# Two expert layers in a two-layer transformer: gates broadcast through DRAM instead of spread by matmuls

## The reference

```
x = x + attention0(layernorm(x))     # 16 heads of 8, rotary
x = x + moe0(layernorm(x))           # one shared and 7 routed experts, top 2, width 352
x = x + attention1(layernorm(x))
x = x + layer1_ffn(layernorm(x))     # relative attention, then 32 experts, top 4, width 128
```

```
# moe0, w[..., e] the normalised softmax gate (1 for the shared expert)
out = out + w[..., e:e+1] * einsum(silu(h @ g.T) * (h @ u.T), d)
# the second expert layer
h   = relu(einsum('bsd,edh->bseh', x2, keys))
out = einsum('bseh,ehd,bse->bsd', h, values, gate)
```

## Time and profile before

| what | us |
|---|---|
| median of 3 runs | 2346.78 (2344.66 to 2352.80) |
| profiled execution | 2339.8 |
| its span, first to last instruction | 2338.0 |
| `experts0`, first key matmul to accumulator copy | 473.4 to 691.7 |
| `experts1`, first spread matmul to accumulator copy | 2116.3 to 2329.3 |
| PE, DVE, ACT, POOL busy | 2140.5, 1581.1, 1303.8, 655.6 |

### The profile page before, as it was taken

How to read it: one execution, slowest core, us unless ns; L and a number is a source line. 1 busy time by engine, 2 the same in 40 slices (tenths; PEclk the granted TensorE clock), 3 DMA queues, 4 the chain that set the end, 5 groups by cost and what they waited for, 6 DMA issues and landing times.

```text
span 2338.0 us, 45544 instructions
## 1 busy us (share of the span) xinstructions
PE 2140.5 (92%) x14816; PEld 1312.2 (56%) x14816; DVE 1581.1 (68%) x2143; ACT 1303.8 (56%) x2269; POOL 655.6 (28%) x596
## 2 busy tenths in 40 slices
PE   4799999599984999999599999999999999959998
PEld 2344444367762344444277777777776777746765
DVE  4899997555545999996665666666666566666665
ACT  1588888155541688888244444444444444425675
POOL 1000000267761000000222222232322222226886
PEclk8799999599996899999699999999999999969999
DMA  7344442200005344442500100000000010100000
GB/s 235 112 117 118 106 121 70 60 30 19 10 0 156 100 111 122 107 117 73 168 13 24 33 26 24 24 24 24 24 24 24 25 34 24 35 28 19 20 20 27
DMA packets 85495, 142.87 MB, mean 61 GB/s; under 512 B 17152, under 2 KB 54016, under 8 KB 85120
## 3 DMA queue, kind: packets, MB, share of 16 engines
q1 hardware_dynamic: 85440, 142.19, 22.5%
HBM read 107.91 MB, written 36.04 MB: 62 GB/s over the span
## 4 chain that ended last, share of the span: by engine, by line
PE 39%; POOL 7%; issue 2%; DVE 2%; DMA 1%; SPq 0%; POOLq 0%; ACT 0%; DVEq 0%
PE PS L696 17%; PE PS L529 10%; POOL BIG_r L1630 7%; PE PS L725 5%; PE PS L691 4%; PE PS L681 2%; DMA rope<-r_dram 0%; PE PS L551 0%; DVE st L897 0%; DVE xn L909 0%; POOLq L1629 0%; SPq L327 0%; DMA Ws_r<-w_stack 0%; DVE BIG L1065 0%; DMA q_stack<-hl 0%
## 5 line engine op out<-in xcount | busy, mean ns | idle before, releaser
L1101 DVE TENSOR_REDUCE M<-PS 128x1 f32<-128x1024 f32 x512 | 605.6, 1220 | 72.3 <-PE PS L595 68.1
L1361 ACT ACTIVATE PR<-PS 128x512 f32<-128x512 f32 x1024 | 536.6, 589 | 121.0 <-PE PS L615 119.0
L1120 DVE TENSOR_REDUCE M<-PS 128x1 f32<-128x1024 f32 x256 | 313.5, 1225 | 235.9 <-PE PS L696 235.9
L615 PE MATMUL PS<-Qs_r,Ks_r 32*128 32x512 f32 x1024 | 369.6, 502 | 1.6 <-ACT PR L1361 1.1
L1389 ACT ACTIVATE BIG<-PS 128x512 f32<-128x512 f32 x256 | 153.0, 598 | 335.0 <-PE PS L529 335.0
L625 PE MATMUL PS<-PR,Va 128*32 128x256 f32 x4096 | 318.8, 396 | 0.0
L595 PE MATMUL PS<-Ks_r,Qs_r 32*128 32x512 f32 x1024 | 266.5, 516 | 44.8 <-DVE hl L1023 17.6
L1378 ACT ACTIVATE PR<-PS,M 128x1024 f32<-128x1024 f32 x256 | 284.9, 1113 | 12.3 <-DVE M L1120 12.3
L615 PEld LDWEIGHTS PS<-Qs_r,Ks_r 32*128 32x128 f32 x1024 | 151.8, 184 | 248.9 <-ACT PR L1361 176.6
L529 PE MATMUL PS<-ident,PR 128*128 128x128 f32 x2080 | 272.2, 274 | 3.7 <-DVE PR L1235 1.9
L529 PEld LDWEIGHTS PS<-ident,PR 128*128 128x128 f32 x2080 | 238.7, 141 | 50.9 <-issue 20.8
(11 more groups left out here) (169 smaller groups left out, 3024.4 us busy)
## 6 DMA issues: line engine op xcount, KB each, us to landing
Qs_r<-q_stack SPq DMA_DIRECT2D x320, 128.0 KB, 2.6
Ks_r<-k_stack SPq DMA_DIRECT2D x320, 128.0 KB, 3.1
o_dram<-Ob SPq DMA_DIRECT2D x96, 128.0 KB, 2.3
q_stack<-hl SPq DMA_DIRECT2D x36, 256.0 KB, 3.0
k_stack<-hl SPq DMA_DIRECT2D x36, 256.0 KB, 3.9
Ks<-in_kv SPq DMA_DIRECT2D x32, 128.0 KB, 2.4
rope<-o_dram SPq DMA_DIRECT2D x24, 128.0 KB, 2.7
rope<-r_dram SPq DMA_DIRECT2D x24, 128.0 KB, 2.8
```

Of the source, the lines that this page charges most:

```text
L615: e.matmul(bank(RING[(x if x < 4 else x + 1) % 3]), Ks_r[rows_, s, kt * P:(kt + 1) * P], Qs_r[rows_, s, qh * GW:(qh + 1) * GW], start=True ...
L1101: e.tensor_reduce(M[:, s, qt:qt + 1], PS[:, 2 + 2 * (qt % 2):4 + 2 * (qt % 2), :] .rearrange("p a b -> p (a b)"), AX.X, ALU.max, negate=Tr ...
L1120: e.tensor_reduce(M[:, s, qt:qt + 1], PS[:, 2 * (qt % 2):2 * (qt % 2) + 2, :] .rearrange("p a b -> p (a b)"), AX.X, ALU.max, negate=True). ...
L1361: e.activation(PR[:, kt % 4, qh * GW:(qh + 1) * GW], bank(RING[(x if x < 4 else x + 1) % 3]), ACT.Exp, scale=SCALE).then_inc(exp_done, 1)
```

## The change

The gates no longer pass through matmuls.

- In the two router fronts the three-way bf16 split is gone. PE transposes the fp32 gates directly ([128 tokens, 32] into [32, 128], 16 times); DVE copies groups 0 and 2 out of PSUM, ACT groups 1 and 3. POOL no longer builds `sel`; its load and a bf16 identity are gone.
- At the head of each expert stage SP writes the four groups to a DRAM tensor `g_dram` [32, 2048], waits for all four, and then loads the row of an expert into all 128 partitions, 1,024 KB for each expert. `experts0` has two such buffers, `experts1` three.
- `experts0`: the spread is gone, and DVE multiplies x by the gate tile in SBUF. The ring of PSUM places has six steps per unit in place of seven, and the order of products changes a little. The two weight casts move from DVE to ACT (after the first unit of an expert); the subtractions stay on DVE.
- `experts1`: the spread and the relu pass are gone. One DVE instruction takes max(key, 0) times gate out of PSUM; for token groups 0 and 1 it writes `hf` in SBUF, for groups 2 and 3 it writes back into the PSUM bank. ACT makes every high part. The low part of groups 0 and 1 is POOL's, that of groups 2 and 3 is DVE's. The weight cast moves to ACT, the weight subtraction to POOL, behind the two low parts of the expert. Each group has a key bank of its own. PE's order stays key(v), value(v-3).

```diff
 # SP
+            def gates_out(k):
+                for g in range(NG):
+                    if g % 2:
+                        e.wait_ge(gt_ok_a, 2 * k + g // 2 + 1)
+                    else:
+                        e.wait_ge(gt_ok, 2 * k + g // 2 + 1)
+                    e.dma_start(g_dram[:, g * GW:(g + 1) * GW], GTs[:, g * GW:(g + 1) * GW]).then_inc(gt_out, 16)
+                e.wait_ge(gt_out, 16 * NG * (k + 1))
+
+            def load_gate(x, s):
+                e.dma_start(gb[s], g_dram[x:x + 1, :].broadcast_to([P, TT * P])).then_inc(gb_in[s], 16)
+
             def experts(k):
-                with e.Fori(0, [NE0, NE1][k] // 2 - 1) as i:
-                    for s in range(2):
-                        e.wait_ge([w0_ok, wsp_ok][k], 2 * i + s + 1)
-                        load_expert(k, 2 * i + s + 2, s)
+                slots = 2 + k
+                gates_out(k)
+                for x in range(slots):
+                    load_gate(x, x)
+                for x in range([NE0, NE1][k] - 2):
+                    e.wait_ge([w0_ok, wsp_ok][k], x + 1)
+                    load_expert(k, x + 2, x % 2)
+                    y = x + 2 if k == 0 else x + 1
+                    if slots <= y < [NE0, NE1][k]:
+                        e.wait_ge([xw_ok, hf_ok][k], NG * (y - slots) + NG)
+                        load_gate(y, y % slots)
 # PE, front
-                        m = e.transpose(bank(g, BF16)[0:ROWS, t * P:(t + 1) * P],
-                                        gsp[:, GT * g + t, :, :].rearrange("p a x -> p (a x)"), identb[:])
+                        m = transpose(PS[0:NE1, g, t * P:(t + 1) * P], gate[:, GT * g + t, :])
 # PE, experts1, unit(i, s, tg); tg == 0 still waits for wsp_ok of its own expert
-                    if not (isinstance(v, int) and v < 2):
-                        e.wait_ge(hf_ok, v - 1)
+                    if not (isinstance(v, int) and v < NG):
+                        if tg >= 2:
+                            e.wait_ge(hlo_ok_d, 2 * (x - 1) + tg - 1)
+                        else:
+                            e.wait_ge(hf_ok, v - 3)
                     cols_ = slice(tg * GW, (tg + 1) * GW)
-                    e.matmul(bank(2 * (tg % 2)), sel[0:ROWS, x, :], GTs[0:ROWS, cols_], start=True, stop=True)
-                    three(bank(2 * (tg % 2) + 1), [wsp[:, s, 0, r, :] for r in range(2)],
+                    three(bank(tg), [wsp[:, s, 0, r, :] for r in range(2)],
                           (XTh[:, cols_], XTl[:, cols_]), True).then_inc(key_ps, 1)
 # DVE, experts0
-                def weights(x, par, k):
-
-                    e.wait_ge(ew_in[par], 32 * (k + 1))
-                    e.wait_ge(dn_ok, count(NG * (x - 1)))
-                    own(e.tensor_copy(wgp[par][:, 0], wg[:, par]))
-                    own(e.tensor_copy(wdp[:, par, 0], wd[:, par]))
-                    own.settle()
+                def weights(x, par):
+
+                    e.wait_ge(whi_ok, x + 1)
                     own(e.tensor_tensor(wgp[par][:, 1], wg[:, par], wgp[par][:, 0].bitcast(F32), ALU.subtract))
-                    e.tensor_tensor(xw[:, tg % 2, :], XT[:, tg * GW:(tg + 1) * GW], bank(b), ALU.mult)\
-                        .then_inc(xw_ok, 1)
+                    e.tensor_tensor(xw[:, tg % 2, :], XT[:, tg * GW:(tg + 1) * GW], gb[par][:, tg * GW:(tg + 1) * GW],
+                                    ALU.mult).then_inc(xw_ok, 1)
 # DVE, experts1
+                def low(x, tg):
+
+                    e.wait_ge(hhi_ok, NG * x + tg + 1)
+                    e.tensor_tensor(hlo[:, tg, :], bank(tg), hhi[:, tg, :].bitcast(F32), ALU.subtract)\
+                        .then_inc(hlo_ok_d, 1)
+
+                def unit(x, tg):
+                    slot, load = (x % 3, 4 + x // 3 + 1) if x % 3 < 2 else (2, x // 3 + 1)
+                    gate_ = gb[slot][:, tg * GW:(tg + 1) * GW]
+                    e.wait_ge(key_ps, NG * x + tg + 1)
+                    if tg == 0:
+                        e.wait_ge(gb_in[slot], 16 * load)
+                    if tg < 2:
+                        if x > 0:
+                            e.wait_ge(hlo_ok, 2 * (x - 1) + tg + 1)
+                        e.scalar_tensor_tensor(hf[:, tg, :], bank(tg), 0.0, gate_, ALU.max, ALU.mult).then_inc(hf_ok, 1)
+                    else:
+                        e.scalar_tensor_tensor(bank(tg), bank(tg), 0.0, gate_, ALU.max, ALU.mult).then_inc(hf_ok, 1)
+
+                for x in range(NE1):
+                    unit(x, 0)
+                    if x > 0:
+                        low(x - 1, 3)
+                    for tg in range(1, NG):
+                        unit(x, tg)
+                    low(x, 2)
+                low(NE1 - 1, 3)
 # ACT, experts1 (in experts0 alike, with two casts, behind the last pass of an expert's first unit)
-                    e.activation(hhi[:, tg, :], hf[:, tg, :], ACT.Copy).then_inc(hhi_ok, 1)
+                    e.activation(hhi[:, tg, :], hf[:, tg, :] if tg < 2 else bank(tg), ACT.Copy).then_inc(hhi_ok, 1)
...
+                    e.activation(wsp[:, s, :, 0, :], we[:, s % 2], ACT.Copy).then_inc(whi_ok, 1)
...
+                    high(v, tg)
+                    if tg == 0 and not (last and s == SLOTS - 1):
+                        weights(SLOTS * i + s + 1, (s + 1) % SLOTS, 2 * i + (s + 1) // 2)
 # POOL, experts1
+                def weights(x, s):
+
+                    e.wait_ge(whi_ok, NE0 + x + 1)
+                    e.tensor_tensor(wsp[:, s, :, 1, :], we[:, s % 2], wsp[:, s, :, 0, :].bitcast(F32), ALU.subtract)\
+                        .then_inc(wsp_ok, 1)
+
+                def expert(x, s, last=False):
+                    for tg in range(2):
+                        e.wait_ge(hhi_ok, NG * x + tg + 1)
+                        e.tensor_tensor(hlo[:, tg, :], hf[:, tg, :], hhi[:, tg, :].bitcast(F32), ALU.subtract)\
+                            .then_inc(hlo_ok, 1)
+                    if not last:
+                        weights(x + 1, (s + 1) % SLOTS)
```

More of the change, by code:

```diff
@@ L746, in zero_acc @@
                     e.matmul(bank(b), acc[:, 0, 0:P], acc[:, 0, :], start=True, stop=True, skip_group_check=True)
-            def spread(x, ring, tg):
-                e.matmul(bank(ring), sel[0:ROWS, x, :], GTs[0:ROWS, tg * GW:(tg + 1) * GW], start=True, stop=True)\
-                    .then_inc(b_ps, 1)
             def three(out, w, h, start):
@@ L776, in up @@
                         [x_parts[r][:, tg * GW:(tg + 1) * GW] for r in range(2)]
[L777 removed]
+                    three(PS[0:w, (6 * tg + place) % 4, :], [wgp[par][:, r, k, lo:lo + w] for r in range(2)], h, True)\
                         .then_inc([g_ps, u_ps][k], 1)
@@ L785, in unit @@
                     up(0, par, tg, 0, 0)
-                    if not (last and tg == NG - 1):
-                        e.wait_ge(h_ok, count(3 * v - 1))
-                        y, t2 = (x, tg + 1) if tg < NG - 1 else (x + 1, 0)
-                        e.matmul(bank((7 * tg + 1) % 4), sel[0:ROWS, y, :], GTs[0:ROWS, t2 * GW:(t2 + 1) * GW],
-                                 start=True, stop=True).then_inc(b_ps, 1)
-                    e.wait_ge(sg_ok, count(3 * v))
-                    if first and tg == 0:
-                        e.wait_ge(xw_ok, 1)
-                    up(2, par, tg, 1, 0)
+                    e.wait_ge(h_ok, count(3 * v - 1))
+                    up(1, par, tg, 1, 0)
                     par2, tg2 = (par, tg - 1) if tg else (1 - par, NG - 1)
@@ L811, in unit @@
                     e.wait_ge(sg_ok, 3 * v + 2)
-                    up(6, par, tg, 2, 1)
-                e.matmul(bank(2), sel[0:ROWS, 0, :], GTs[0:ROWS, 0:GW], start=True, stop=True).then_inc(b_ps, 1)
+                    up(5, par, tg, 2, 1)
                 for tg in range(NG):
@@ L1199, in experts1 @@
                 e.memset(acc[:, 0, :], 0.0).then_inc(acc_zero, 1)
-                def weights(x, s, k):
-                    e.wait_ge(ew_in[s % 2], 16 * (NE0 + k + 1))
-                    if not (isinstance(x, int) and x < SLOTS):
-                        e.wait_ge(val_ok, NG * (x - SLOTS + 1))
-                    own(e.tensor_copy(wsp[:, s, :, 0, :], we[:, s % 2]))
-                    own.settle()
-                    e.tensor_tensor(wsp[:, s, :, 1, :], we[:, s % 2], wsp[:, s, :, 0, :].bitcast(F32), ALU.subtract)\
-                        .then_inc(wsp_ok, 1)
@@ L1220, in experts1 @@
-                weights(0, 0, 0)
-                for s in range(SLOTS):
-                    for tg in range(NG):
-                        unit(0, s, tg)
-                with own.loop(NE1 // SLOTS - 2, SLOTS) as i:
-                    for s in range(SLOTS):
-                        for tg in range(NG):
-                            unit(i + 1, s, tg)
-                for s in range(SLOTS):
-                    for tg in range(NG):
-                        unit(NE1 // SLOTS - 1, s, tg, True)
+                def low(x, tg):
+                    e.wait_ge(hhi_ok, NG * x + tg + 1)
```

(23 more changed lines are left out.)

153 lines of the change are left out of this document (65 added, 88 removed).

## The result

The changed kernel took 2309.74 us, the median of 4 runs (2307.15 to 2311.02), against 2349.25 (2344.66 to 2352.80) for the kernel before: a ratio of 0.9832, 95% interval 0.981 to 0.9853. The forecast was 2328.4, range 2313 to 2345. The direction was right and the size was not: the time lies 18.7 us under the forecast and 3.3 us under the range.

What follows compares the result with a forecast made beforehand. PE's instruction count was taken to bound both expert stages. Gains of 9.7 us in `experts1` and 8.7 in `experts0`, 18.4 together, taken from 2346.8 gave 2328.4 us, range 2313 to 2345.

Steps and rivals of the forecast that it cites:

- the period of the loop: `experts1`: each expert's start hangs on the one before, through DVE, ACT and POOL; 6.17 us per expert, against 6.56 before.
- the start of `experts1`: Gate 0 lands at 2119.55; with 1.5 us charged for a clock fall, expert 1 starts in effect at 2126.1.
- the start of `experts0`: First gated product at 478.4 instead of 476.92: 1.5 us lost, and 1.5 more for a fall of the clock.
- the stalls at the split: `experts0`: 7 PE waits of about 1.0 us for DVE's multiply behind the weight split; 4.5 of 7 us gained.
- the offset: The median of the kernel before lies 7.0 us above its profiled execution; carried over to the changed kernel.
- Removed spreads: `experts0` loses 31 spread matmuls of 0.2314 us inside the stage: 7.2 us gained.
- The gate read: Loading an expert's 1,024 KB gate row takes 5.6 us, 7.7 at the upper end; sets the loop's pace from 6.6.
- The tail: End of `experts1`: 8.4 us from the start of expert 31 to the accumulator copy.
- Nothing: `experts1`: writes back to PSUM cost nothing, being outside the loop; the cast goes to ACT, where 3 us are free.
- PE-bound after all: Rival: `experts1` runs at PE's own 5.56 us an expert, 18.3 us more gained, 2310; chance 0.08.
- Gate loads late: Rival: gate loads on the slow side; 2349 us if a load takes 7.7, 2371 at 9; chance 0.15.
- The clock did not fall in the loop: Rival: the clock falls in the steady loop, where PE idles 0.6 of 6.2 us; 11.1 an expert, 2476; chance 0.03.

Runs made afterwards that it cites:

- p3: The changed kernel with the two weight casts of each expert in `experts0` back on DVE; 2317.33 us.
- p5: The changed kernel with 18 extra matmuls on PE in `experts0` while it waits for the first gated product; 2310.37 us.
- p1: The changed kernel with POOL's weight subtraction in `experts1` moved between the two low parts instead of behind them; 2291.36 us.
- p2: The changed kernel with each gate row in `experts1` loaded a second time, into an unread spare buffer, ahead of the real load; 2331.69 us (one run).
- r3: The changed kernel run again with no edit; 2307.95 us.
- q5: The changed kernel with 9 extra matmuls on PE in `experts0` while it waits for the first gated product; 2313.39 us (one run).

## Why the prediction missed

The mechanism was right, in both stages and in the loop; what failed are sizes, nearly all to the same side: the period of the loop (5.7 us), the start of `experts1` (4.8), the start of `experts0` (2.7 net of the clock), the stalls at the split (1.7) and the offset (4.4). The 18.7 us are: 10.6 from `experts1`, 4.4 from `experts0`, less 0.8 in the stages that nothing changes, and 4.4 from the offset (7.0 carried over, 2.6 found; both against the first medians).

- **Removed spreads.** Forecast 7.2 us in `experts0`. Units take 6.25 against 6.48 before, as forecast: right.
- **The stalls at the split.** I took 4.5 of 7 us because DVE and POOL lock each other out. The lock is there (549 to 1646 ns), but all 7 stalls went. From the first gated product to the copy the kernel gained 214.8 - 201.4 = 13.4 us at full clock, where spreads and stalls together had been put at 11.7: 1.7 us too little. What failed is the step from a slower instruction to a late multiply; my own sum had given "between 1 us and 2.4 us late, against 1.85 of slack", and the true case lay inside the slack. p3 shows that moving the casts was the cause of about three quarters of it.
- **Start of `experts0`.** Forecast + 17.6 for the first gated product, measured + 14.6. The writes began 0.6 us earlier and took 3.1 us from the first issue to the last landing, not 4.4 (issued 0.44 apart and not 0.6, landed in 1.7 and not 2.3); the read took 4.5, not 5.6. The clock cost 1.8 and not 1.5. Together 3.0 + 1.7 - 0.3 = 4.4.
- **The gate read.** The estimate of L = 5.6 came from 287 GB/s in a stretch in which two experts' weights were loaded. The changed kernel moves 430 GB/s while gates load (columns as before), and the read takes 4.3 to 4.7 us.

```profile
2106.00:2108.00 2.00, 0.96 (x3) 0.48 (x3) 1.47 (x3) 1.44 (x3) 2.00 (x2) 1.00 1.02 430
```

  The Trainium skill, "DMA: Bandwidth & Descriptors", Anatomy of one DMA, gives about 2.0 us and 436 GB/s for a DMA issued by GpSimd, an estimate of 4.4 us here. This trace, with reads issued by SyncE, is near it: 4.5 and 4.3 us at the two starts, 4.7 in the median. I had set it aside for a row with other transfers, in which a DMA share of 0.92 moved 287 GB/s.
- **Start of `experts1`.** Expert 1 was to start in effect at gates + 21.3, it started at + 16.5 (2108.96): 4.8 us, 1.6 for the read's issue (+ 7.5, not + 9.1), 1.3 for the read, 0.3 for the chain behind it, and 1.5 for a fall of the clock that did not happen, since PE was still at keys when the gate landed. That was luck of the execution: PE was late because it had zeroed at half clock for part of the time; in p3 and p5, where it had not, the fall came. So charging it was no error of the forecast.
- **The loop.** Forecast 6.17, measured 5.98 over 30 experts: 5.7 us. Link by link: PE to DVE 1.00 for 1.11; DVE's three 1.37 to the start of the third and 0.80 to ACT, 2.17 for 2.24; the last three links 2.83 for 2.82. The first I had taken from the earlier trace rows, where DVE wakes for a copy after the last product. The second: instructions of 0.69 us on DVE start 0.61 apart when they follow each other, but only the second did. The third started 0.76 behind it, because the key of group 1 was ready no sooner (its last matmul ends at 2200.94, the third instruction starts at 2200.98):

```profile
2200.22 0.68 DVE L1204 TENSOR_TENSOR BIG_r<-PS,BIG_r 128x512 fp32r<-128x512 f32 x1
...
2200.32 0.62 PE L768 MATMUL PS<-Ah,PR_r 128*128 128x512 f32 x2
```

  The forecast had put that key at nothing, since it was to be ready before DVE was free: DVE was free earlier than forecast, and this link of the loop is PE's and not DVE's. The first three experts took 5.85, the later ones 6.00; why ACT's handover grew from 0.73 to 0.80 is open.
- **The tail** took 8.3 for 8.4.
- **Nothing** was charged for the writes back to PSUM and for ACT's casts, and nothing showed: 0.700 us instead of 0.692 for the former, and ACT was busy for 85.6 of 186 us in the steady loop.
- **Rivals.** The measured 2309.7 is the number of "PE-bound after all" (2310), and that is chance: its period of 5.56 did not come, because POOL's order stood in the way; p1 shows that it is one line away, and there the price is 5.44 and not 5.56. "Gate loads late" did not come, with up to 2 us to spare (p2). The clock did not fall in the loop: 1.00 in the stretch that holds the waits. The range's low end had the loop, the stalls, the read and the clock in it, and those came, but for the clock in `experts0` (1.8 lost); it left out the writes ahead of the read (2.0 and 1.6 us at the two starts) and the offset (4.4).

## What to carry over

When each round of a loop waits for a chain through several engines, write down the order on every engine of the chain and ask which instruction stands ahead of the one that the next round needs: moving one 0.74 us instruction ahead of a 1.29 us one was worth 16 us, beside 37 to 40 for the whole change. Price a write, read back and first use by rows of like transfers; the rate of another kind of transfer misled by 1.1 to 1.3 us each time. And do not carry an offset between one profiled execution and a median over to another kernel before looking at the granted clock of both.

## What the runs showed of the hardware

- The moment at which the clock rises in a front differs between executions of the same code: eight zeroing matmuls took 3.67, 5.38 (the changed kernel) and 6.64 us. The kernel before lay between 2338.8 and 2349.9 us in 30 runs, and the longer ones had for the most part the lower mean granted clock (0.945 to 0.935).
- At the start of `experts1` the clock fell to 0.50 where TensorE had been idle for 3.4 to 3.5 us (p1, p3, p5) and stayed at 1.00 where it had been idle for 1.2 to 1.5 (the changed kernel, r3, q5). The earlier rise of the clock brought the longer idle time, so a faster zeroing gained nothing there.
- DVE instructions of 0.68 to 0.69 us start 0.61 us apart when nothing is waited for, and POOL's of 1.29 start 1.25 apart. Sums of durations overstate a packed engine by an eighth on DVE and by 3% on POOL.
- DVE reading and writing the same PSUM bank costs 0.700 us per 128x512, against 0.692 to SBUF.
- An 8 KB row of DRAM read into all 128 partitions (1 MB) lands in 4.7 us (4.2 to 8.4), a quarter of it in 3.3.
